# Attention in a gated transformer layer: probabilities stored as byte pairs, unpacked by GpSimd, which also forms the row minimum

## The reference

```python
q = _fq_sym(q, axis=-1); k = _fq_sym(k, axis=-1); v = _fq_sym(v, axis=2)   # to 127 steps
attn = jnp.einsum('bhqd,bhkd->bhqk', q, k)
attn = jax.nn.softmax(attn.astype(jnp.float32), axis=-1)
attn = _fq_unsigned(attn, axis=-1)      # s = max/255; round(attn/s) in 0..255, times s
out = jnp.einsum('bhqk,bhkd->bhqd', attn, v)
```

## Time and profile before

| | |
|---|---|
| median of 3 runs | 2253.66 us |
| the profiled execution | 2256.53 us, its span 2254.5 us, mean granted clock 0.652 |
| attention, first to last piece on DVE | from 441.0 us to about 1864 us |
| busy over the span | DVE 1895.3 us (84%), PE 1729.1 (77%), ACT 1377.3 (61%), POOL 233.0 (10%) |

### The profile page before, as it was taken

One profiled execution on the slowest core, in us unless ns is written; L12 is line 12 of the kernel. 1 busy time (PEld: TensorE's weight loads), 2 busy tenths in 40 slices (PEclk: granted clock), 3 DMA queues, 4 the chain that ended last, 5 costly groups with the idle time before them and its releaser, 6 DMA issues. The chain is left out here.

```text
span 2254.5 us, 35460 instructions
## 1 busy us (share of the span) xinstructions
PE 1729.1 (77%) x12800; PEld 838.6 (37%) x12800; DVE 1895.3 (84%) x3044; ACT 1377.3 (61%) x1294; POOL 233.0 (10%) x157
## 2 busy tenths in 40 slices
PE   7899996188787878878878878878877885853656
PEld 3455553033343333333433434334333343321323
DVE  6798888699898889889979979979988994738887
ACT  4344444076676767767767767767766772377771
POOL 0122223200000000000000000000000004315331
PEclk9999998555555555555555555556556557966878
DMA  6433332499999999999999999999999996100001
GB/s 210 157 95 109 106 98 65 114 204 201 210 205 206 211 193 209 212 194 208 207 196 213 204 198 210 205 208 199 204 209 198 206 203 186 38 1 0 19 19 38
DMA packets 1121188, 359.05 MB, mean 159 GB/s; under 512 B 1061376, under 2 KB 1094656, under 8 KB 1119104
## 3 DMA queue, kind: packets, MB, share of 16 engines
q1 hardware_dynamic: 1120448, 355.26, 81.4%
q0 software_dynamic: 576, 1.57, 0.2%
HBM read 65.27 MB, written 23.07 MB: 39 GB/s over the span
## 5 line engine op out<-in xcount | busy, mean ns | idle before, releaser
L740 DVE TENSOR_SCALAR_CACHE_REDUCE att_scaled<-att_scores,layer_nsq 128x1536 f32<-128x1536 f32 (+1 forms) x768 | 1221.8, 1637 | 163.8 <-PE att_scores L714 126.1
L759 ACT ACTIVATE att_probs<-att_scaled,att_bias_row 128x4096 uint16<-128x4096 f32 x256 | 949.5, 3709 | 442.2 <-DVE att_low_log L745 442.2
L714 PE MATMUL att_scores<-att_k_head,att_q_head 96*128 96x512 bf16 x2048 | 977.3, 605 | 254.9 <-DVE att_scaled L740 171.0
L723 PEld LDWEIGHTS att_ps_o<-att_v_head,att_probsT 128*128 128x128 f16 x8192 | 389.3, 111 | 494.8 <-issue 459.0
L723 PE MATMUL att_ps_o<-att_v_head,att_probsT 128*128 128x32 bf16 x8192 | 370.5, 191 | 73.6 <-DMA att_probsT<-att_probs 67.8
L714 PEld LDWEIGHTS att_scores<-att_k_head,att_q_head 96*128 96x128 bf16 x2048 | 175.1, 117 | 449.4 <-DVE att_scaled L740 250.2
L855 POOL TENSOR_TENSOR mix_scaled<-layer_o_sum,mix_p_step 128x512 f32 (+1 forms) x16 | 21.0, 1310 | 1473.6 <-DVE mix_p_step L931 1473.6
L487 PE MATMUL kv_ps_v<-kv_weights_wkv,kv_inT 128*128 128x512 f32 x256 | 117.8, 603 | 0.0
L491 PE MATMUL kv_ps_k<-kv_weights_wkv,kv_inT 128*128 128x512 f32 x256 | 115.1, 592 | 0.0
L1066 PE MATMUL ffn_ps_h<-layer_w1T,layer_ints_T 128*128 128x512 bf16 x256 | 66.4, 424 | 32.9 <-DVE ffn_pre L1239 31.8
L1079 PE MATMUL ffn_ps_t<-layer_ident,ffn_upped 128*128 128x128 f16 x256 | 25.0, 274 | 81.7 <-DVE ffn_upped L1218 71.3
(11 more groups left out here) (140 smaller groups left out, 1526.1 us busy)
## 6 DMA issues: line engine op xcount, KB each, us to landing
k_parts<-kv_k_stage SPq DMA_DIRECT2D x16, 768.0 KB, 5.2
att_k_head<-k_parts SPq DMA_DIRECT2D x16, 768.0 KB, 6.0
q_w_in<-in_L_ffn_w_dram SPq DMA_DIRECT2D x32, 256.0 KB, 3.4
kv_weights_ctx_in<-in_ctx_dram SPq DMA_DIRECT2D x32, 256.0 KB, 3.3
kv_weights_w_in<-in_L_ffn_w_dram SPq DMA_DIRECT2D x32, 256.0 KB, 2.6
att_q_head<-q_ints SPq DMA_DIRECT2D x48, 128.0 KB, 6.1
q_x_in<-in_x_dram SPq DMA_DIRECT2D x16, 256.0 KB, 3.0
v_ints<-kv_v_int SPq DMA_DIRECT2D x4, 1024.0 KB, 5.2
```

Of the source, the lines that this page charges most:

```text
L714: last = pe.matmul(buffer[:, x:x + 512], q_head[slot][:, at:at + P], k_head[slot][:, STARTS[j] + x:STARTS[j] + x + 512], start=True, stop= ...
L723: last = pe.matmul(ps_o[r % 2][:, 0:D], probsT[r % T_BUFS][:, k, :].bitcast(FP16), v_head[r // QT][:, k * D:(k + 1) * D], start=(k == 0), ...
L740: dve.tensor_scalar(scaled[u][:, STARTS[j]:STARTS[j] + WIDTHS[j]], scores[(s * NCH + j) % 2][:, 0:WIDTHS[j]], kept["nsq"][:, ds(g, 1)], No ...
L759: act.activation(probs[s % R_BUFS][:, :], scaled[u][:, :], ACT.Exp, bias=bias_row[:, u:u + 1], scale=-1.0, accum_out=den[:, ds(g, 1)]).the ...
```

## The change

- `probs` (uint16, 4096 wide, 4 buffers) becomes `pairs` (uint16, 2048 wide, 2 buffers). ACT writes bytes: key c of the first half of the keys goes to the even byte of pair c, key c of the second half to the odd byte. Its output is a two-dimensional pattern with a step of two bytes.
- The DMA transpose is of 128×2048 uint16 to `pairsT` (2 buffers): half the bytes. It waits for the unpacking of the unit two before.
- GpSimd unpacks `pairsT` in four pieces of 1024 elements (uint8 with a step of two bytes to bf16) to `probsT` (bf16, 4 buffers), two units behind (`C_LAG`).
- The minimum over the three pieces and the addition of log 255 move from DVE to GpSimd, as two small `tensor_scalar` instructions ahead of the unpacking in each step. `low` and the bias have three buffers, `scaled` three.
- PE multiplies bf16 instead of fp16 bits, five units behind; it waits for `probs_ready` (four per unit). ACT copies the result ahead of its exponential instead of behind, without the scale 2^24, also five units behind.
- DVE, ACT and GpSimd are written out for all 256 units; PE keeps its loop.

```diff
-        R_BUFS = 4
-        T_BUFS = 4
+        S_BUFS = 3
+        R_BUFS = 2
+        T_BUFS = 2
+        C_BUFS = 4
+        PIECES = 4
+        HALF = KT // 2
...
+        pairs = [c.sb(f"pairs{i}", [P, KEYS // 2], U16) for i in range(R_BUFS)]
+        pairsT = [c.sb(f"pairsT{i}", [P, HALF, P], U16) for i in range(T_BUFS)]
+        probsT = [c.sb(f"probsT{i}", [P, KT, P], BF16) for i in range(C_BUFS)]
...
-        V_LAG, O_LAG = 4, 4
+        C_LAG = 2
+        V_LAG, O_LAG = 5, 5
...
                 load(0, 0, 0)
                 for g in range(UNITS):
-                    step(g, g % UNROLL)
+                    b = g % T_BUFS
+                    after(sp, probs_ready, (g - T_BUFS + 1) * PIECES)
+                    sp.wait_ge(pairs_ready, g + 1)
+                    sp.dma_start_transpose(pairsT[b][:, :, :], pairs[g % R_BUFS][:, :]).then_inc(pairs_turned[b], 16)
+                    if g % QT == QT // 2 and live(g + QT, UNITS):
+                        load(g // QT + 1, (g // QT + 1) % 2, g - QT // 2)
...
-                                pe.wait_ge(probs_turned[r % T_BUFS], (g - V_LAG - r % T_BUFS) * (16 // T_BUFS) + 16)
+                                pe.wait_ge(probs_ready, (g - V_LAG) * PIECES + PIECES)
...
             @block.vector
             def _(dve):
+                for g in range(UNITS):
+                    u = g % S_BUFS
+                    after(dve, pairs_ready, g - S_BUFS + 1)
                     for j in range(NCH):
...
-                    dve.wait_ge(scaled_ready, g * NCH + NCH)
-                    dve.tensor_scalar(low_log[:, :], low[u][:, :], LOG255, None, ALU.add, ALU.min,
-                                      accum_out=bias_row[:, u:u + 1]).then_inc(row_ready, 1)
-
-                pipelined(dve, UNITS, UNROLL, V_LAG, step)
+            @block.gpsimd
+            def _(pool):
+                def lowest(g):
+                    u = g % S_BUFS
+                    pool.wait_ge(scaled_ready, (g + 1) * NCH)
+                    after(pool, row_ready, g)
+                    pool.tensor_scalar(low_row[:, :], low[u][:, 0:1], low[u][:, 1:2], low[u][:, 2:3],
+                                       ALU.min, ALU.min).then_inc(low_ready, 1)
+                    pool.wait_ge(low_ready, g + 1)
+                    pool.tensor_scalar(bias_row[:, u:u + 1], low_row[:, :], 1.0, LOG255, ALU.mult, ALU.add).then_inc(row_ready, 1)
+
+                def unpack(g):
+                    b = g % T_BUFS
+                    pool.wait_ge(pairs_turned[b], (g // T_BUFS + 1) * 16)
+                    after(pool, pv_ready, g - C_BUFS + 1)
+                    for piece in range(PIECES):
+                        parity, first = piece // 2, (piece % 2) * (HALF // 2)
+                        turned = pairsT[b][:, first:first + HALF // 2, :].rearrange("p k q -> p (k q)").bitcast(U8)
+                        pool.tensor_copy(probsT[g % C_BUFS][:, parity * HALF + first:parity * HALF + first + HALF // 2, :]
+                                         .rearrange("p k q -> p (k q)"),
+                                         turned.rearrange("p (n two) -> p two n", two=2)[:, parity, :]).then_inc(probs_ready, 1)
+
+                for g in range(UNITS + C_LAG):
+                    if live(g, UNITS):
+                        lowest(g)
+                    if live(g - C_LAG, UNITS):
+                        unpack(g - C_LAG)
 
             @block.scalar
             def _(act):
+                for g in range(UNITS + O_LAG):
+                    if live(g - O_LAG, UNITS):
+                        r = g - O_LAG
+                        act.wait_ge(pv_ready, r + 1)
+                        act.copy(o_sum[:, (r % QT) * C + (r // QT) * D:(r % QT) * C + (r // QT + 1) * D],
+                                 ps_o[r % 2][:, 0:D]).then_inc(o_kept, 1)
                     if live(g, UNITS):
+                        u = g % S_BUFS
                         act.wait_ge(row_ready, g + 1)
 
                         if live(g - R_BUFS, UNITS):
+                            act.wait_ge(pairs_turned[g % T_BUFS], (g // T_BUFS) * 16)
+                        act.activation(pairs[g % R_BUFS][:, :].bitcast(U8).rearrange("p (c two) -> p two c", two=2),
+                                       scaled[u][:, :].rearrange("p (two c) -> p two c", two=2), ACT.Exp,
+                                       bias=bias_row[:, u:u + 1], scale=-1.0, accum_out=den[:, g:g + 1]).then_inc(pairs_ready, 1)
```

More of the change, by code:

```diff
@@ L11 @@
 U16 = mybir.dt.uint16
+U8 = mybir.dt.uint8
 ALU = mybir.AluOpType
@@ L649, in attend @@
         v_head = [c.sb(f"v_head{i}", [P, KT * D], BF16) for i in range(2)]
[L650 to L655, removed]
+        scaled = [c.sb(f"scaled{i}", [P, KEYS], F32) for i in range(S_BUFS)]
+        pairs = [c.sb(f"pairs{i}", [P, KEYS // 2], U16) for i in range(R_BUFS)]
+        pairsT = [c.sb(f"pairsT{i}", [P, HALF, P], U16) for i in range(T_BUFS)]
+        probsT = [c.sb(f"probsT{i}", [P, KT, P], BF16) for i in range(C_BUFS)]
+        low = [c.sb(f"low{i}", [P, NCH], F32) for i in range(S_BUFS)]
+        low_row = c.sb("low_row", [P, 1], F32)
+        bias_row = c.sb("bias_row", [P, S_BUFS], F32)
         scores = [c.ps(f"scores{i}", [P, WIDEST], F32) for i in range(2)]
@@ L662, in attend @@
         scaled_ready = c.sem("scaled_ready")
+        low_ready = c.sem("low_ready")
         row_ready = c.sem("row_ready")
+        pairs_ready = c.sem("pairs_ready")
+        pairs_turned = [c.sem(f"pairs_turned{i}") for i in range(T_BUFS)]
         probs_ready = c.sem("probs_ready")
-        probs_turned = [c.sem(f"probs_turned{i}") for i in range(T_BUFS)]
         pv_ready = c.sem("pv_ready")
@@ L720, in step @@
                                 after(pe, o_kept, g - V_LAG - 1)
-                                pe.wait_ge(probs_turned[r % T_BUFS], (g - V_LAG - r % T_BUFS) * (16 // T_BUFS) + 16)
+                                pe.wait_ge(probs_ready, (g - V_LAG) * PIECES + PIECES)
                             for k in range(STARTS[j] // P, (STARTS[j] + WIDTHS[j]) // P):
-                                last = pe.matmul(ps_o[r % 2][:, 0:D], probsT[r % T_BUFS][:, k, :].bitcast(FP16),
+                                last = pe.matmul(ps_o[r % 2][:, 0:D], probsT[r % C_BUFS][:, k, :],
                                                  v_head[r // QT][:, k * D:(k + 1) * D], start=(k == 0), stop=(k == KT - 1))
@@ L731, in _ @@
             def _(dve):
[L732 to L736, removed]
+                for g in range(UNITS):
+                    u = g % S_BUFS
+                    after(dve, pairs_ready, g - S_BUFS + 1)
                     for j in range(NCH):
                         dve.wait_ge(scores_ready, g * NCH + (j + 1))
-                        dve.tensor_scalar(scaled[u][:, STARTS[j]:STARTS[j] + WIDTHS[j]], scores[(s * NCH + j) % 2][:, 0:WIDTHS[j]],
-                                          kept["nsq"][:, ds(g, 1)], None, ALU.mult, ALU.min,
+                        dve.tensor_scalar(scaled[u][:, STARTS[j]:STARTS[j] + WIDTHS[j]], scores[(g * NCH + j) % 2][:, 0:WIDTHS[j]],
+                                          kept["nsq"][:, g:g + 1], None, ALU.mult, ALU.min,
@@ L750, in _ @@
             @block.scalar
             def _(act):
-                def step(g, s):
+                for g in range(UNITS + O_LAG):
[4 more added lines that the diff above has]
+                                 ps_o[r % 2][:, 0:D]).then_inc(o_kept, 1)
                     if live(g, UNITS):
-                        u = s % 2
+                        u = g % S_BUFS
@@ L755, in step @@
                         act.wait_ge(row_ready, g + 1)
                         if live(g - R_BUFS, UNITS):
[L758 to L766, removed]
@@ L768, in _ @@
-                pipelined(act, UNITS, UNROLL, O_LAG, step)
+                            act.wait_ge(pairs_turned[g % T_BUFS], (g // T_BUFS) * 16)
+                        act.activation(pairs[g % R_BUFS][:, :].bitcast(U8).rearrange("p (c two) -> p two c", two=2),
+                                       scaled[u][:, :].rearrange("p (two c) -> p two c", two=2), ACT.Exp,
+                                       bias=bias_row[:, u:u + 1], scale=-1.0, accum_out=den[:, g:g + 1]).then_inc(pairs_ready, 1)
```

## The result

The changed kernel takes 2163.8 us (median of 4 runs, 2159.1 to 2165.7) against 2254.6: a ratio of 0.959 (95% interval 0.957 to 0.961), 91 us less. The forecast was 65 us less, 2189 us, range 2172 to 2390: the direction held, and so did most of the mechanism; the time lies 8 us under the range.

The account below looks back on a forecast made before the run. It took the ring over two PSUM score buffers (5.24 us a unit) as the bound, plus stalls at head loads and loop jumps. 41 + 19 + 4 + 4.5 + 1.5 − 5 = 65 us gave 2189 us, range 2172 to 2390.

Parts of the forecast that it names:

- The unit's ring and its 5.2 us: DVE's piece 0 and piece 1, then release and PE's matmuls, over two PSUM score buffers: 5.24 us a unit.
- GpSimd's copy: Unpacking on GpSimd: 0.85 ns an element, 1.00 us per piece of 1024, 4.0 us a unit, hidden.
- Transposes: DMA transposes with half the bytes: issue from 4.94 to about 2.5 us, 4.8 us to landing.
- The end of the stage: From the last minimum to the last copy: 14.6 us instead of 16, a gain of 1.5.
- Stalls: Gains booked: 41 us behind head loads, 19 at DVE's loop jumps, 4 for late transposes before jumps, less 5.
- The 5 us: Given back from the 41 us booked for head-load stalls, for what may spill.
- The split of the stalls: Head-load stalls 41 us and late transposes before jumps 4; DVE's own six loop jumps 19 us.
- the 24 booked for jumps and registers: Written-out DVE and ACT: 19 us for DVE's six jumps, 4.5 us for its register instruction.
- 0.3 us left: SP's spare time before the change: issuing a transpose takes 4.94 us, under the unit's 5.24.
- I assume that the clock stays at its half: PE's clock: no rise assumed, so moving the minimum off DVE gains nothing in a steady unit.
- The range: 8 in 10 for 2172 to 2390 us, leaving out rival 1's slow half and a little below.
- rival 1: GpSimd's four unpacking copies become the bound from 1.03 ns an element: 2366 us at 1.25, 2570 at 1.48; chance 0.22.

Follow-up runs that it names:

- a7: The changed kernel with PE written out too and scores in four pieces of 1024 in three PSUM buffers: 2107.9 us, ratio 0.935.
- a10: The changed kernel without the loads of heads 2 to 15: 2160.8 us, ratio 0.959.
- b1: The kernel before with DVE's and ACT's streams written out instead of looped, nothing else: 2241.6 us, ratio 0.993.
- c1: b1 without the loads of heads 2 to 15, all heads computed from the first two heads' data: 2177.0 us, ratio 0.965.
- a1: The changed kernel with the row minimum put back on DVE, GpSimd only unpacking: 2162.3 us, ratio 0.958.
- a6: The changed kernel with a fifth copy of 1024 elements per unit on GpSimd, into a spare buffer: 2312.4 us, ratio 1.026.
- a8: a7 with the row minimum put back on DVE: 2120.3 us (median of three), ratio 0.942.

## Why the prediction was wrong, step by step

- *The unit's ring and its 5.2 us*: right. A step is 5.21 us, the idle before piece 0 is ended by PE, and a7, which takes the ring away, goes to 4.82.
- *GpSimd's copy*: forecast 1.00 us per 1024 elements, measured 1.04 by itself and 1.00 in a row. The two places of the Trainium skill that the prediction cites (GPSIMD Engine Reference) part here. By § 3.1's loop of about 1.8 cycles, which that section doesn't say is one-input work as the prediction has it, a copy would be 1.5 us, an estimate. The trace bears out § 4.1's "roughly line-rate": DVE's pieces of 1024 take 1.28 us each, GpSimd's copies 1.04. The minimum costs 0.7 and not 0.5 us (its first instruction, with two operands by pointer, 0.36); the unit is 4.7 instead of 4.5 us, still hidden.
- *Transposes*: forecast 2.5 us an issue and 4.8 to landing, measured 1.9 and 4.3. ACT's bytes with a step of two cost nothing: 3712 ns against 3709.
- *The end of the stage*: forecast 14.6 us, measured 14.4 (1771.8 to 1786.2).
- *Stalls*: booked 41 + 19 + 4, less 5 that might spill: 59 us. Measured 69.8 (87.8 before, 18.0 after, and these are PE's six jumps). The 5 us were caution and a10 shows that nothing spills. The other 6 are a term sized too small: I took the stalls as what the stage had over 255 × 5.24, from which the fast steps of before and the loop's register time had already been netted.
- *The split of the stalls* into 45 for late transposes and 19 for jumps was wrong, though the sum nearly held. They weren't two causes side by side: a head was bound by its transfers, and the jumps were partly hidden in that. Written out alone gives 15 us (b1) of the 24 booked for jumps and registers; the rest of the change, bytes above all, gives 78 (2241.6 to 2163.8). I saw "0.3 us left" per transpose and didn't multiply it by 16 and hold it against a load of 7 us.
- *"I assume that the clock stays at its half"*: this step failed, and it put the clock's term of the sum at nothing without a reason, though the PEclk line of the earlier trace rows has three sixes among the stage's fives. The full-clock share of the stage doubled (6% to 13%; 0.53 to 0.56 in the mean), and the fast steps, each of which overlaps such a stretch, give 18.3 us. The new number format isn't needed for it: taking the loads away from b1 (c1) raises the granted clock from 0.54 to 0.59 with the old one, as high as in a1, which has the new one. What makes the chip grant the clock stays open; PE's busy share of the stage doesn't order the runs (79% in a6 as in a7, at 0.51 and 0.66). I had thought of the clock only as something that would make the minimum's move matter; in a1 the two offset each other.
- *The range* leant on the slow side for GpSimd, and its low end allowed 17 us over the forecast's gain. The clock alone takes those: in the profiled pair, 97.4 us apart, 32 us are missed, of which 18 are fast steps, 6 the stall term, 5 the spill and 3 lie outside the stage (395.1 us from the last unit to the end of the span before, 390.3 after, where I had booked 1.5). The medians lie 91 us apart, 26 over the forecast; how their missing 6 us spread over these terms no trace shows.
- *A slip that nothing hangs on*: rival 1's own formula, with 0.1 us of fixed part, reaches 5.24 us at 1.06 ns an element; the 1.03 of the text goes with 0.13.

## What to carry over

Multiply an engine's spare time per unit by the units between two disturbances and compare it with the disturbance: if it is less, that engine or queue is the bound over the period, however idle it looks in a unit, and stalls of other kinds are hidden in it. When the clock is granted in stretches, a change of the stage can also change how much of it runs at full clock (0.50 to 0.70 in the runs here); give that a bound instead of assuming it away. And an edit that relieves an engine outside the ring is worth nothing until the ring is cut, and then lands on whichever engine has the least left (here GpSimd at 4.7 of 4.8 us).

## What the runs showed of the hardware

- GpSimd turns uint8 with a step of two bytes into bf16 at 1.00 us per 1024 elements on 128 partitions, beside DVE, whose PSUM reads keep it busy some 90% of the stage: 1037 to 1050 ns by itself over 1024 copies, and no different in the last twelve, which ran when DVE had finished (1037 to 1049).
- A 128×1 `tensor_scalar` with two pointer operands takes 0.36 us on GpSimd, one with immediates 0.19.
- At the half clock PE was busy 96% of a stage (1236.8 of 1287.5 us, a8, granted clock 0.50); in a7, whose PE waits for GpSimd's late unpacking behind the same scores, it was 0.66.
